# Moving the softmax broadcast matmul behind the next block's first score matmuls, and sharing the feature-major writes between two queues

## The chip, the cores and the metric

The kernel runs on the 8 cores of one Trainium2 chip (two dies, cores 0 to 3 and 4 to 7). The four sequences of the batch are spread over four pairs of cores; each core computes 2048 of the 4096 rows of its sequence, through both layers. No core waits for another. The time is device microseconds of the slowest core.

## The reference, cut to what matters

```python
# x: (4, 4096, 4096)
# attention: 32 heads of 128, 8 key/value heads; every linear is y = x @ sign(W).T * mean|W|
scores = einsum('bhqd,bhkd->bhqk', q, k) / sqrt(128)
attn = softmax(scores, axis=-1)
out = einsum('bhqk,bhkd->bhqd', attn, v)
x = layernorm(x + bitnet_linear(out, o_weight, o_scale))
# feed forward: a base linear and a gated LoRA (8 experts, top 2)
x = layernorm(x + base(x) + 2.0 * lora(x))
```

## The kernel before

The program is a list of stages, each a block in which all engines start together. Stage 1 loads and transposes x. Stage 2 is the Q projection, stage 3/4 the K and V projections, stage 5 the attention, stage 6 the output projection, stage 7 a layernorm, stage 8 the gate and the base linear, stage 9 the last layernorm. Order within a stage is written out by hand with semaphores.

**Attention (`phase5`).** The work is 32 heads times 4 query tiles of 512, which makes 128 blocks, numbered i. Four heads share a key/value head. In a block TensorE goes through 16 steps p of 256 keys. A step issues two score matmuls (line 1123, into one half of the four PSUM banks PSQ), then, for the step before, two value matmuls (line 1217, accumulated in PSA) and two column sums (line 1223, stationary operand a column of ones, accumulated in row 0 of PSD). ScalarE turns each step's scores into a bf16 tile of exponentials (line 1191, three tiles PT in turn). When the last column sum is done, ScalarE computes 1/sum as exp(-ln(sum)) in two small instructions (lines 1195 and 1197), TensorE spreads this row over 128 partitions with a matmul against a row of ones (line 1140, written into PSD as well), VectorE copies the result out of PSD (line 1169) and multiplies PSA by it (line 1171), and GpSimd issues the write to AOUT (line 1205). At the end of a head, VectorE then copies the next head's softmax offset `sm_negu` out of the first half of PSB (line 1176); the first exponential of a new head waits for that copy (`sNg`).

Semaphores of the boundary between blocks: `sPV` counts column sums, `sRc` the reciprocals, `sBc` the broadcast matmuls, `sAo` the products of line 1171, `sEx` the exponentials, `sQK` the score pairs. The first value matmul of a block waits for `sAo` of the block before, because it overwrites PSA. TensorE executes in the order in which the code issues: the score matmuls of block i+1 stand behind the broadcast of block i.

**Layernorm (`emit_ln`).** It runs over 16 tiles of 128 rows. SyncE loads the projection's output and the residual (lines 1260 and 1261) two tiles ahead, once the tile before in the same buffer has been normalized and its write has landed. VectorE adds (1269), takes statistics (1276, 1273, 1279, 1281), waits for ScalarE's square root (1307) and normalizes (1289). In stage 7 only (`fm_out`), ScalarE then casts the tile to bf16 (1312), TensorE transposes it in 32 pieces (1328), VectorE copies four groups of eight out of PSUM (1298), and GpSimd issues one write of the tile to X1TM (1357) and 32 writes of 32 KB each, rows of 256 bytes, to X1FM (1342). Stage 8 begins by loading X1FM (1394), when all of stage 7 is done.

Of the kernel before, what the change touches and what calls it, by code (L numbers as in the profile page):

```python
# [10 lines left out]
AF = mybir.ActivationFunctionType  # L11
# [7 lines left out]
H = 32  # L19
HK = 8  # L20
HD = 128
ND = 32
NTS = 32
NT = 16
# [1036 lines left out]
def phase5(c):  # L1061
# [25 lines left out]
    with nc.Block() as blk:  # L1087
# [16 lines left out]
        def _(t):  # L1104
# [3 lines left out]
            for kvh in range(HK):  # L1108
                bk = kvh % 2
                sKV.wait(t, kvh, per=32)  # L1110
                for r in range(4):
# [3 lines left out]
                    for qt in range(NQT):  # L1115
                        i = h * 4 + qt
                        for p in range(NP):
# [9 lines left out]
                            last.then_inc(sQK, 1)  # L1127
                            if p >= 1:
                                _p5_pvden(c, t, i, p - 1, bk, VBUF, PT, psa, psd,
                                          sEx, sPV, sAo)  # L1130
                            if qt == 3 and p == 4 and h + 1 < H:
# [5 lines left out]
                        _p5_pvden(c, t, i, NP - 1, bk, VBUF, PT, psa, psd, sEx, sPV, sAo)  # L1137
                        t.wait_ge(sRc, i + 1)
                        t.wait_ge(sAo, i)
                        t.matmul(psd[:, 0:512], c.sm_ones_row.ap(),  # L1140
                                 c.sm_recb.ap(), start=True, stop=True).then_inc(sBc, 1)
# [38 lines left out]
        def _(s):  # L1180
            for h in range(H):
                for qt in range(NQT):
# [12 lines left out]
                    sc_(c, s.activation(c.sm_recl.ap(), psd[0:1, 0:512], AF.Ln))  # L1195
# [15 lines left out]
def _p5_pvden(c, t, i, p, bk, VBUF, PT, psa, psd, sEx, sPV, sAo):  # L1211
    t.wait_ge(sEx, NP * i + p + 1)
    if p == 0:
        t.wait_ge(sAo, i)
    for u in range(2):
        cc = 2 * p + u
        t.matmul(psa[:, 0:512], VBUF[bk][:, cc * 128:(cc + 1) * 128],  # L1217
                 PT[p % 3][:, u * 512:(u + 1) * 512],
                 start=(cc == 0), stop=(cc == 31))
    last = None  # L1220
    for u in range(2):
        cc = 2 * p + u
        last = t.matmul(psd[0:1, 0:512], c.sm_ones_col.ap(),  # L1223
                        PT[p % 3][:, u * 512:(u + 1) * 512],
                        start=(cc == 0), stop=(cc == 31))
    last.then_inc(sPV, 1)


def emit_ln(c, name, in_a_dram, in_b_getter, out_writer, fm_out):
# [7 lines left out]
    sCst = _sem(c, name + "_cs")  # L1237
    sTp = _sem(c, name + "_tp")
    sEv = _sem(c, name + "_ev")
    sFd = DSem(c, name + "_fd")  # L1240
# [9 lines left out]
    with nc.Block() as blk:  # L1250
# [13 lines left out]
        def _(v):  # L1264
            for tc in range(NT):
# [25 lines left out]
                if fm_out:  # L1291
                    for g in range(4):
# [3 lines left out]
                        if tc >= 2 and g == 0:  # L1296
                            sFd.wait(v, tc - 2, per=512)
# [5 lines left out]
        def _(s):  # L1303
            for tc in range(NT):
# [3 lines left out]
                if fm_out:  # L1308
# [3 lines left out]
                    s.activation(XB16[b], XB[b], AF.Copy).then_inc(sCst, 1)  # L1312

# [20 lines left out]
        def _(g):  # L1334
            for tc in range(NT):
# [3 lines left out]
                if fm_out:  # L1339
                    g.wait_ge(sEv, 4 * (tc + 1))  # L1340
                    for dc in range(ND):
# [5 lines left out]
            if fm_out:  # L1347
                sFd.wait(g, NT - 2, per=512)
                sFd.wait(g, NT - 1, per=512)
# [184 lines left out]
```

## Time and profile before

| | us |
|---|---|
| median of 2 runs | 10725.3 |
| the two runs | 10706.13 and 10744.47 |
| the profiled execution, its own time | 10707.58 |
| its span, slowest core (core 6) | 10706.0 |
| spans of cores 0 to 3 | 10611.9 to 10621.7 |
| spans of cores 4 to 7 | 10689.9 to 10706.0 |

In the profile PE is TensorE's matmuls, PEld its weight loads, DVE is VectorE, ACT is ScalarE, POOL is GpSimd, SP is SyncE. An engine's busy time on matmuls is modelled, so a busy PE is not PE at its peak. [...] TensorE's matmuls are busy for 76% of the span, ScalarE is busy for 29%, VectorE for 22%, GpSimd for 12%. Times of rows are microseconds from the start of the span of core 6.

### The profile page before, as it was taken

The page shows a single profiled execution, that of the slowest core. Times are in us where ns is not written, and L with a number is a line of the kernel's source. Part 1 is how long each engine was busy: PE and PEld are TensorE (multiplying, and loading weights), DVE is VectorE, ACT ScalarE, POOL GpSimd, SP SyncE. Part 2 cuts the span into 40 slices and gives each one's busy share as a digit, 9 for nine tenths or more (in the row PEclk, how much of TensorE's full clock was granted, in tenths as well). Part 3 has the DMA queues.
Part 4 walks back from the last instruction along what each step waited for, and adds up shares of the span by engine and source line. Part 5 has one row for each costly group of instructions (what it writes and reads, how often), then busy time and mean ns, then how long its engine had stood idle before and what let it go on. Part 6 is the DMA issues. An engine that isn't in the chain of part 4 may idle for free. (4 is left out here: it accounts for less than half of the span.)

```text
span 10706.0 us, 101056 instructions; the slowest of 8 cores (10611.9 to 10706.0 us)
## 1 busy us (share of the span) xinstructions
PE 8146.9 (76%) x35416; PEld 3093.4 (29%) x36044; DVE 2334.5 (22%) x4091; ACT 3083.4 (29%) x2857; POOL 1233.8 (12%) x2278
## 2 busy tenths in 40 slices
PE   3688884888878888888888888867777612899960
PEld 2344432333321111111111111124444311444430
DVE  3344435122210000000000000013333263122226
ACT  3211102000036666665565666620000010111100
POOL 0000000222210000000000000001111173122210
PEclk6799995988888888887888888878888855999975
DMA  9422214111100000000000000032222284222238
GB/s 300 149 69 69 69 56 137 42 42 42 42 27 17 8 17 9 19 16 8 17 8 17 8 17 11 6 104 71 71 71 71 84 304 170 93 83 83 83 115 299
DMA packets 186183, 782.94 MB, mean 73 GB/s; under 512 B 47850, under 2 KB 48226, under 8 KB 158818
## 3 DMA queue, kind: packets, MB, share of 16 engines
q1 hardware_dynamic: 100130, 541.40, 16.0%
q0 software_dynamic: 85568, 235.03, 5.9%
q8 instruction: 310, 5.08, 0.2%
q14 instruction: 175, 1.43, 0.0%
HBM read 541.36 MB, written 234.89 MB: 73 GB/s over the span
## 5 line engine op out<-in xcount | busy, mean ns | idle before, releaser
L552 PE MATMUL PSQ<-BIG 128*128 128x512 bf16 x12000 | 2759.8, 391 | 27.3 <-issue 15.0
L1191 ACT ACTIVATE BIG<-PSQ,sm_negu 128x1024 bf16<-128x1024 f32 x2048 | 2265.7, 1113 | 1364.0 <-PE PSQ L1123 1277.3
L552 PEld LDWEIGHTS PSQ<-BIG 128*128 128x128 bf16 x12288 | 1239.1, 101 | 1532.3 <-issue 265.3
L1217 PE MATMUL PSA<-BIG 128*128 128x512 bf16 x3982 | 1317.4, 412 | 199.4 <-ACT BIG L1191 190.6
L1123 PE MATMUL PSQ<-BIG 128*128 128x512 bf16 x3964 | 1342.5, 428 | 27.1 <-issue 15.1
L523 ACT ACTIVATE BIG<-BIG 128x1024 bf16<-128x1024 f32 x384 | 398.2, 1054 | 3340.0 <-PE PSB L539 2501.4
L1223 PE MATMUL PSD<-BIG,sm_ones_col 128*1 128x512 bf16 x4096 | 1313.6, 404 | 11.1 <-issue 2.7
L1169 DVE CAST BIG<-PSD 128x512 bf16<-128x512 f32 x128 | 88.5, 691 | 3786.6 <-PE PSD L1140 3786.6
L1217 PEld LDWEIGHTS PSA<-BIG 128*128 128x128 bf16 x4096 | 312.3, 101 | 984.6 <-issue 934.7
L539 PE MATMUL PSB<-sm_idb,BIG 128*128 128x128 bf16 x3072 | 259.6, 247 | 401.6 <-DVE BIG L583 310.5
L1123 PEld LDWEIGHTS PSQ<-BIG 128*128 128x128 bf16 x4096 | 257.1, 101 | 968.9 <-issue 960.0
L1205 POOL DMA_DIRECT2D AOUT<-BIG x128 | 69.0, 539 | 3926.4 <-DVE BIG L1171 3893.9
L1223 PEld LDWEIGHTS PSD<-BIG,sm_ones_col 128*1 128x1 bf16 x4096 | 174.9, 81 | 986.2 <-issue 986.2
L928 PE MATMUL PSQ<-BIG 128*128 128x512 bf16 x1024 | 406.2, 397 | 12.7 <-DMA BIG<-XFM 8.3
L636 POOL DMA_DIRECT2D OOUT<-BIG x512 | 271.4, 538 | 1208.7 <-DVE BIG L738 1171.5
L932 PE MATMUL PSQ<-BIG 128*128 128x512 bf16 x1024 | 403.4, 394 | 2.7 <-issue 0.4
L636 POOL DMA_DIRECT2D FFOUT<-BIG x512 | 271.4, 538 | 1150.4 <-DVE BIG L738 1106.4
L926 PE MATMUL PSQ<-BIG 128*128 128x512 bf16 x976 | 387.4, 397 | 4.9 <-DVE BIG L986 4.8
L930 PE MATMUL PSQ<-BIG 128*128 128x512 bf16 x981 | 387.2, 395 | 0.0
L1191 ACT ACT_TABLE_LOAD x1 | 1.3, 1283 | 1264.8 <-PE PSQ L1123 1264.8
L539 PEld LDWEIGHTS PSB<-sm_idb,BIG 128*128 128x128 bf16 x3072 | 221.1, 111 | 447.1 <-issue 427.2
L1328 PE MATMUL PSB<-sm_idb,BIG 128*128 128x128 bf16 x512 | 59.2, 308 | 339.3 <-ACT BIG L1312 336.9
(167 smaller groups left out, 4954.7 us busy)
## 6 DMA issues: line engine op xcount, KB each, us to landing
BIG<-x SPq DMA_DIRECT2D x48, 2048.0 KB, 15.3
BIG<-wq SPq DMA_DIRECT2D x128, 512.0 KB, 5.5
BIG<-wo SPq DMA_DIRECT2D x128, 512.0 KB, 5.3
BIG<-wb SPq DMA_DIRECT2D x128, 512.0 KB, 5.3
XFM<-BIG POOLq DMA_DIRECT2D x32, 1024.0 KB, 14.9
BIG<-XFM SPq DMA_DIRECT2D x32, 1024.0 KB, 4.7
OOUT<-BIG POOLq DMA_DIRECT2D x512, 64.0 KB, 1.9
BIG<-OOUT SPq DMA_DIRECT2D x16, 2048.0 KB, 9.4
```

The lines of the kernel that those rows point to most:

```text
L523: P.inc(s.activation(WSG[i % 4], WST[i % 4], func), "sg")
L539: last = t.transpose(pb[:, j * 128:(j + 1) * 128], WSG[i % 4][:, j * 128:(j + 1) * 128], c.sm_idb.ap())
L552: last = t.matmul(psq[:, qt * 512:(qt + 1) * 512], WT[bdo][:, dc, :], c.RES[:, dc, qt * 512:(qt + 1) * 512], start=(dc == 0), stop=(dc == ...
L636: g.dma_start(out_dram.ap()[tc, :, do * 128:(do + 1) * 128], OSTG[b][:, j * 128:(j + 1) * 128]).then_inc(sDm.h(oq), 16)
L926: t.matmul(psq[:, 0:512], lhs, WKT[:, dc, 0:512], start=(dc == 0), stop=(dc == ND - 1))
L928: t.matmul(psq[:, 512:1024], lhs, WKT[:, dc, 512:1024], start=(dc == 0), stop=(dc == ND - 1))
L930: t.matmul(psq[:, 1024:1536], lhs, WVT[:, dc, 0:512], start=(dc == 0), stop=(dc == ND - 1))
L932: lastmm = t.matmul(psq[:, 1536:2048], lhs, WVT[:, dc, 512:1024], start=(dc == 0), stop=(dc == ND - 1))
L1123: last = t.matmul(psq[:, (cc % 4) * 512:(cc % 4) * 512 + 512], KBUF[bk][:, cc * 128:(cc + 1) * 128], QBUF[bq][:, qt * 512:(qt + 1) * 512], ...
L1191: s.activation(PT[p % 3], psq[:, bank:bank + 1024], AF.Exp, bias=c.sm_negu.ap()[:, h % 2:h % 2 + 1]).then_inc(sEx, 1)
L1217: t.matmul(psa[:, 0:512], VBUF[bk][:, cc * 128:(cc + 1) * 128], PT[p % 3][:, u * 512:(u + 1) * 512], start=(cc == 0), stop=(cc == 31))
L1223: last = t.matmul(psd[0:1, 0:512], c.sm_ones_col.ap(), PT[p % 3][:, u * 512:(u + 1) * 512], start=(cc == 0), stop=(cc == 31))
```

## The change

In attention the broadcast matmul of block i is issued after the first two score matmuls of block i+1, and only the last block keeps it at its end. The column sums move from row 0 of PSD to row 0 of the second half of PSB, from where ScalarE now reads them; the first value matmul of a block gets one more wait, for the reciprocal of the block before, because the column sums that follow overwrite that row. The broadcast still goes to PSD.

In stage 7 the 32 writes of a tile to X1FM are shared: GpSimd issues the even ones and ScalarE, on its own queue and after its cast of the tile and VectorE's four copies, the odd ones. ScalarE's have a semaphore pair of their own (`sFd2`).

```diff
@@ phase5, TensorE
                             last.then_inc(sQK, 1)
+                            if p == 0 and i >= 1:
+                                t.wait_ge(sRc, i)
+                                t.wait_ge(sAo, i - 1)
+                                t.matmul(psd[:, 0:512], c.sm_ones_row.ap(),
+                                         c.sm_recb.ap(), start=True,
+                                         stop=True).then_inc(sBc, 1)
                             if p >= 1:
                                 _p5_pvden(c, t, i, p - 1, bk, VBUF, PT, psa, psd,
-                                          sEx, sPV, sAo)
+                                          sEx, sPV, sAo, sRc)
...
-                        t.wait_ge(sRc, i + 1)
-                        t.wait_ge(sAo, i)
-                        t.matmul(psd[:, 0:512], c.sm_ones_row.ap(),
-                                 c.sm_recb.ap(), start=True, stop=True).then_inc(sBc, 1)
+                        if i == H * NQT - 1:
+                            t.wait_ge(sRc, i + 1)
+                            t.wait_ge(sAo, i)
+                            t.matmul(psd[:, 0:512], c.sm_ones_row.ap(),
+                                     c.sm_recb.ap(), start=True,
+                                     stop=True).then_inc(sBc, 1)
@@ phase5, ScalarE
-                    sc_(c, s.activation(c.sm_recl.ap(), psd[0:1, 0:512], AF.Ln))
+                    sc_(c, s.activation(c.sm_recl.ap(), c.psbf[0:1, 512:1024], AF.Ln))
@@ _p5_pvden
     if p == 0:
         t.wait_ge(sAo, i)
+        if i >= 1:
+            t.wait_ge(sRc, i)
...
-        last = t.matmul(psd[0:1, 0:512], c.sm_ones_col.ap(),
+        last = t.matmul(c.psbf[0:1, 512:1024], c.sm_ones_col.ap(),
@@ emit_ln, ScalarE
                     s.activation(XB16[b], XB[b], AF.Copy).then_inc(sCst, 1)
+                    s.wait_ge(sEv, 4 * (tc + 1))
+                    for dc in range(1, ND, 2):
+                        s.dma_start(c.X1FM.ap()[dc, :, tc * 128:(tc + 1) * 128],
+                                    XSTG[b].rearrange("p (a b) -> p a b", a=32)[:, dc, :]
+                                    ).then_inc(sFd2.h(tc), 16)
@@ emit_ln, GpSimd
-                    for dc in range(ND):
+                    for dc in range(0, ND, 2):
                         g.dma_start(c.X1FM.ap()[dc, :, tc * 128:(tc + 1) * 128],
...
```

## Rows read from the trace of the kernel before

**Rows 1.** Busy time of attention: stretch, us, engines' busy (x count), PEclk, DMA share, GB/s.
```profile
3070.00:6990.00 3920.00, 3482.29 (x12010) 747.12 (x12253) 181.01 (x343) 2384.59 (x2269) 67.41 (x125) 0.87 0.04 13
```
**Rows 2.** Line 1195, one per block: duration min/median/max, first and last start.
```profile
L1195 ACT ACTIVATE BIG<-PSD x128: 586/586/587, 3104.7 to 7049.5; 1x512 f32<-1x512 f32 x128
```
**Rows 3.** Timeline: start, us, instruction [idle before <-releaser], boundary inside a head.
```profile
3283.94 0.59 ACT L1195 ACTIVATE BIG<-PSD 1x512 f32<-1x512 f32 x1 [1.36 <-PE PSD L1223]
...
3285.49 0.37 PE L1140 MATMUL PSD<-BIG,sm_ones_row 1*128 1x512 bf16 x1 [1.65 <-ACT BIG L1197]
3285.80 1.06 PE L1123 MATMUL PSQ<-BIG 128*128 128x512 bf16 x4
...
3286.55 2.12 ACT L1191 ACTIVATE BIG<-PSQ,sm_negu 128x1024 bf16<-128x1024 f32 x2 [1.31 <-PE PSQ L1123]
3286.90 0.69 DVE L1171 TENSOR_TENSOR BIG<-PSA,BIG 128x512 bf16<-128x512 f32 x1
...
3287.92 1.01 PE L1217 MATMUL PSA<-BIG 128*128 128x512 bf16 x2 [1.07 <-ACT BIG L1191]
```
**Rows 4.** Timeline, boundary between two heads.
```profile
3190.88 0.59 ACT L1195 ACTIVATE BIG<-PSD 1x512 f32<-1x512 f32 x1 [1.36 <-PE PSD L1223]
...
3194.75 2.12 ACT L1191 ACTIVATE BIG<-PSQ,sm_negu 128x1024 bf16<-128x1024 f32 x2 [2.56 <-DVE sm_negu L1176]
...
3196.12 1.01 PE L1217 MATMUL PSA<-BIG 128*128 128x512 bf16 x2 [2.34 <-ACT BIG L1191]
```
**Rows 5.** Busy time of five blocks, from one line 1195 to the next.
```profile
3104.70:3132.80 28.10, 24.82 (x95) 5.48 (x97) 1.38 (x2) 18.91 (x18) 0.54 (x1) 1.00 0.02 5
3132.80:3162.70 29.90, 26.22 (x95) 5.75 (x97) 1.58 (x4) 18.97 (x19) 0.54 (x1) 0.94 0.02 5
3162.70:3190.90 28.20, 24.73 (x96) 5.60 (x98) 1.38 (x2) 18.88 (x19) 0.54 (x1) 1.00 0.07 23
3190.90:3222.70 31.80, 27.03 (x95) 5.74 (x97) 1.45 (x3) 18.96 (x19) 0.54 (x1) 0.89 0.02 6
...
3284.00:3314.70 30.70, 27.30 (x96) 5.96 (x98) 1.38 (x2) 18.85 (x19) 0.54 (x1) 0.89 0.07 18
```
**Rows 6.** Busy time within the block of rows 3.
```profile
3287.30:3294.10 6.80, 6.18 (x15) 1.25 (x16) 0.29 (x1) 2.84 (x4) 0.54 (x1) 0.54 0.05 19
```
**Rows 7.** Busy time of one attention block and of two stretches of attention.
```profile
5789.10:5823.00 33.90, 30.18 (x101) 6.62 (x103) 1.45 (x3) 19.85 (x19) 0.54 (x1) 0.81 0.22 82
4774.00:5103.00 329.00, 294.08 (x937) 64.41 (x956) 14.42 (x27) 186.23 (x178) 5.39 (x10) 0.78 0.05 16
5739.00:5898.00 159.00, 142.76 (x464) 31.18 (x472) 7.38 (x15) 92.00 (x89) 2.69 (x5) 0.80 0.06 21
```
**Rows 8.** Timeline of a tile of stage 7.
```profile
8708.62 3.62 ACT L1312 ACTIVATE BIG<-BIG 128x4096 bf16<-128x4096 f32 x1 [3.20 <-DVE BIG L1289]
...
8712.81 0.54 POOL L1357 DMA_DIRECT2D X1TM<-BIG  x1
...
8716.48 0.69 DVE L1298 COPY BIG<-PSB 128x1024 bf16<-128x1024 bf16 x1 [0.16 <-PE PSB L1328]
8717.71 18.89 POOL L1342 DMA_DIRECT2D X1FM<-BIG  x32 [4.36 <-DVE BIG L1298]
8718.27 4.42 DVE L1269 TENSOR_TENSOR BIG<-BIG 128x4096 f32<-128x4096 f32 x1 [1.10 <-DMA BIG<-x]
...
8728.48 0.20 ACT L1307 ACTIVATE sm_sd<-sm_var 128x1 f32<-128x1 f32 x1 [16.24 <-DVE sm_var L1281]
```
**Rows 9.** Waits in stage 7: who waited for whom, us in total, times, longest.
```profile
DVE BIG L1269 <- DMA BIG<-x: 38.5, 12, 25.9
```
**Rows 10.** Lines 1260 and 1394, issues on the SP queue: ns min/median/max.
```profile
L1260 SPq DMA_DIRECT2D BIG<-OOUT x16: 326/327/424, 8541.2 to 8888.0; - x16
L1394 SPq DMA_DIRECT2D BIG<-X1FM x32: 327/1106/3383, 8949.9 to 8986.1; - x32
```
**Rows 11.** Timeline, end of stage 7.
```profile
8926.02 17.08 POOL L1342 DMA_DIRECT2D X1FM<-BIG  x32 [2.76 <-DVE BIG L1298]
```

More of the change, by code:

```diff
@@ L1136, in _ @@
                                          start=True, stop=True).then_inc(sBm, 1)
-                        _p5_pvden(c, t, i, NP - 1, bk, VBUF, PT, psa, psd, sEx, sPV, sAo)
-                        t.wait_ge(sRc, i + 1)
-                        t.wait_ge(sAo, i)
-                        t.matmul(psd[:, 0:512], c.sm_ones_row.ap(),
-                                 c.sm_recb.ap(), start=True, stop=True).then_inc(sBc, 1)
+                        _p5_pvden(c, t, i, NP - 1, bk, VBUF, PT, psa, psd,
+                                  sEx, sPV, sAo, sRc)
+                        if i == H * NQT - 1:
[4 more added lines that the diff above has]
+                                     stop=True).then_inc(sBc, 1)
         @blk.vector
@@ L1208, in _, with _p5_pvden @@
             sAd.wait(g, H * NQT - 1)
-def _p5_pvden(c, t, i, p, bk, VBUF, PT, psa, psd, sEx, sPV, sAo):
+def _p5_pvden(c, t, i, p, bk, VBUF, PT, psa, psd, sEx, sPV, sAo, sRc):
     t.wait_ge(sEx, NP * i + p + 1)
@@ L1236, in emit_ln @@
     sOd = DSem(c, name + "_od")
[L1237 to L1240, printed above, removed]
+    if fm_out:
+        sCst = _sem(c, name + "_cs")
+        sTp = _sem(c, name + "_tp")
+        sEv = _sem(c, name + "_ev")
+        sFd = DSem(c, name + "_fd")
+        sFd2 = DSem(c, name + "_fd2")
+    else:
+        sCst = sTp = sEv = sFd = sFd2 = None
     big1f = c.BIG1.ap().bitcast(F32)
@@ L1296, in _ @@
                         if tc >= 2 and g == 0:
-                            sFd.wait(v, tc - 2, per=512)
+                            sFd.wait(v, tc - 2, per=256)
+                            sFd2.wait(v, tc - 2, per=256)
                         v.tensor_copy(XSTG[b].rearrange("p (a b) -> p a b", a=32)
@@ L1347, in _ @@
             if fm_out:
-                sFd.wait(g, NT - 2, per=512)
-                sFd.wait(g, NT - 1, per=512)
+                sFd.wait(g, NT - 2, per=256)
+                sFd.wait(g, NT - 1, per=256)
+                sFd2.wait(g, NT - 2, per=256)
+                sFd2.wait(g, NT - 1, per=256)
 def phase7(c):
```

## The prediction

> **What bounds the kernel now.** I read the granted clock and busy time by stretch first. Attention takes 3.9 of the 10.7 ms, and its mean granted clock is only 0.87 [rows 1]. TensorE issues 96 matmuls in each block, and line 1195, which runs once per block, starts first at 3104.7 and last at 7049.5 [rows 2]. That is 3944.8 us over 127 blocks, 31.06 us each.
>
> The timeline of a boundary shows what interrupts TensorE. Counted from the start of line 1195, the broadcast starts at +1.55, after 1.65 us of idle. The four score matmuls of two steps run from +1.86. The first value matmul starts at +3.98, after another 1.07 us of idle, and its releaser is the exponential of step 0 [rows 3].  At a boundary between heads the first exponential waits for `sm_negu`, starts at +3.87 instead of +2.61, and the first value matmul starts at +5.24 [rows 4].
>
> The reader should then look at what the pause costs beyond itself. Two blocks ran wholly at 1.00 and took 28.1 and 28.2 us. One at a mean of 0.94 took 29.9. Those at 0.89 took 30.7, or 31.8 at a head boundary [rows 5]. [...] What TensorE did before the fall was to run four large matmuls in 4.2 us. So a boundary costs about 2.5 us through the clock (30.7 less 28.2), beside its waits. All but a handful of the 128 boundaries look like this: at 28.1 us each the 127 blocks would take 3569 us, not 3945.
>
> On this core there is a third kind of block. In 488 us of attention the mean was 0.78 and 0.80, and a block took 33.9 us [rows 7], which makes some 14 blocks 3.3 us longer than the others. That is 46 us, over half of the 84 us by which core 6 ends after the last of cores 0 to 3 (the table above).
>
> **The broadcast moved.** In TensorE's order the score pair of step 0 now comes ahead of the broadcast, right behind the last column sums. Nothing in its own waits holds it back: all exponentials it needs are done. It takes half of the 1.06 us that four score matmuls take [rows 3] and lies in what was 1.65 us of idle. The broadcast itself waits for the same reciprocal, so it stays at +1.55. Behind it only one score pair is left, then the first value matmul.
>
> The first exponential can now start when ScalarE has finished the reciprocal, a little before the broadcast, at about +1.35 instead of +2.61, and it lasts 1.1 us. But the value matmul also waits for `sAo`, since it overwrites PSA. The product of line 1171 starts at +2.96 and lasts 0.69, so it ends at +3.65 [rows 3], and its chain (reciprocal, broadcast, copy, product) is untouched. In this block the value matmul started 0.33 us after that. An engine wakes 0.16 us after its releaser at the shortest [rows 8], and after the exponential TensorE took some 0.3. So the direct gain here is 0.03 to 0.17 us, not the 1.3 us by which the exponential is earlier. [...] The bounds are 0 and 0.5 us; I take 0.2. At the 31 head boundaries the chain through line 1176 stands as it was, and I take 0. Direct gain: 96 blocks by 0.2 is 19 us.
>
> **What the clock makes of it.** The large matmuls of a boundary are the same four, but two of them now join the burst before it. The stretch without a large matmul before the broadcast shrinks from 1.96 us (the last column sum ended 1.65 us before the broadcast, the score matmuls start at +1.86) to about 1.4, while the one before the value matmul grows from 1.07 to about 1.4. The rows show that the fall is not certain even before: of the first three boundaries, all with the same pauses, two had none [rows 5]. Where the stretch of 4.2 us is better filled at its front, more boundaries should pass without a fall, and those that fall should do so later, when TensorE is already in its dense work again and can leave the low level sooner, as the block at 0.94 did. [...] The bounds for one inner block are 0 (all fall as now) and 2.5 us (30.7 less 28.2, none falls). I take one half without a fall (2.5) and one half with the short one (30.7 less 29.9, 0.8), a mean of 1.65 us. This includes most of the direct gain. At head boundaries TensorE idles 2.34 us before the value matmul [rows 4] as before, and I take no gain. Of the 96 inner blocks about 11 lie in the stretches of rows 7, where I take nothing either. That leaves 85 by 1.65, which is 140 us.
>
> **The sums' new row** costs nothing: the same matmuls write another bank, and the added wait for `sRc` is already met when the broadcast has gone. Its cover is the broadcast's own wait; without that it would be the 1.3 us of the reciprocal, which cannot come after it.
>
> **The shared writes of stage 7.** A tile has a cycle of 23 us, set by VectorE. GpSimd needs 18.89 us to issue 32 writes. This delays the next tile's X1TM write: it is issued at 8712.81, though ScalarE had the normalized tile at 8708.62, and the loads that wait for it come late: VectorE waited 1.10 us in this tile [rows 8]. All such waits of the stage are 38.5 us, of which 25.9 are the first tile's, leaving 12.6 [rows 9]. With 16 writes GpSimd is free 9.4 us earlier, so I take 10 of them. At the end the last 32 writes are issued from 8926.02 to 8943.1, [rows 11], and stage 8's loads start at 8949.9 [rows 10]; half of the issuing goes, 8 us.
>
> On ScalarE the 16 issues go between the last copy (end 8717.17) and the square root at 8728.48 [rows 8], 11.3 us in which ScalarE was idle. Behind them waits exactly that square root, and VectorE for it. No row shows an issue by ScalarE. The nearest are SyncE's: 0.33 us each, where few are under way, and a median of 1.11 for 32 in a row of 512 KB each [rows 10]. With about 0.05 between two issues that makes 6 or 18.5 us. I take the low end, since these writes are 32 KB; then nothing is late. At the high end each tile is 7.2 us late. Stage 7: minus 18 us.
>
> [...]
>
> **Sum.** 10,707.6 (the profiled execution) less 140 less 18 is 10,550. That execution lies 18 us under the median of the two runs, 10,725.3, and their spread is 38 us.
>
> **Rivals.**
> - *Every boundary falls as before (0.20).* For it: the same four large matmuls in the same 4.2 us, and VectorE's chain holds the value matmul near +3.9. Against: 2 of 3 early boundaries passed. Left are 19 us and stage 7's 18: 10,670.
> - *No inner block falls (0.18).* 85 by 2.5 is 213, and stage 7's 18: 10,477, over 2% faster than the median.
> - *ScalarE's issues are slow (0.09).* 7.2 us for 15 tiles is 108 us on top of 10,550, less the 10 that are no longer gained: 10,668.
> - *The third level spreads (0.10), the slower side.* Denser work on all cores of the die makes blocks like that of rows 7 more frequent. Each costs 33.9 less 29.2, some 4.7 us against a block of the new kind. From 30 more of them on, the 140 us are gone. If half of all blocks are such, 50 more, the time is 10,785. For it: 0.81 appears on this core in 488 us of attention already. Against: it fills only an eighth of attention, and blocks shortened from 30.7 to 29 us are denser by no more than 6%. [...]
> - *The forecast (0.43).*
>
> **Range and chances.** 2% is about what a measurement of this kernel tells from no change, here 215 us, so faster begins at 10,511. The range is 10,455 to 10,705: it takes in the first three rivals and leaves out most of the fourth and the edges. The forecast's own range is 10,490 to 10,610. Faster: the 0.18 and a tenth from the forecast's lower edge, 0.26. Slower by over 2% would need 10,940, some 80 blocks at the third level: 0.03. Within 2%: 0.71.
>
> **What would show it.** In the profile after: line 1171, not line 1191, releases the first value matmul inside a head, and its start is about +3.9 after line 1195. Blocks of 28 us at a mean of 1.00 stand between others of 29.5 to 30 us; the mean granted clock of attention rises from 0.87 to 0.92 or so, and line 1195's first and last start lie some 3800 us apart. In stage 7 VectorE hardly waits for loads, ScalarE's last issue ends before the next square root is due, and from the stage's start to line 1394 there are about 18 us less. What would make it wrong: a clock that still falls in each block, or stretches at 0.81 over more than a third of attention.

## The result and the profile after

| us | before | after |
|---|---|---|
| median | 10768.26 (9 runs) | 10707.67 (11 runs) |
| lowest and highest | 10701.34 and 10994.81 | 10552.39 and 10860.95 |
| profiled execution, span of its slowest core | 10706.0 (core 6) | 10551.1 (core 1) |
| attention on that core, first to last logarithm | 3944.8 | 3788.5 |
| stage 7 on that core, first addition to the first load of stage 8 | 392.3 | 438.8 |

The ratio of after to before is 0.9833, with a 95% interval of 0.978 to 0.9885; it is taken over the fast runs alone, those in which no die lagged behind the other and whose time lay near the kernel's fastest, while the medians of the table are over all runs (their ratio is 0.9944). Even that ratio is not all the change's. All nine runs of the kernel before took over 10,700 us, and its profiled execution spent time at the clock level of 0.81 [rows 7]. Core 1 of that execution had no such time and took 10,621.7 us, the kernel's fastest later runs took 10,621.6 to 10,628.7, and four of after's eleven took 10,552.4 to 10,558.9, a ratio of 0.9935. So of the 1.7% about 0.65% is shown to be the change itself; the rest most likely goes with that level.

The logarithm, once per block (columns: duration ns min/median/max, first and last start), stands for [rows 2]: 3788.5 us over 127 blocks, 29.83 each, where there were 31.06.

```profile
L1204 ACT ACTIVATE BIG<-PSB x128: 586/586/587, 3107.8 to 6896.3; 1x512 f32<-1x512 f32 x128
```

Busy time by stretch of after (us, PE, PEld, DVE, ACT, POOL with counts, PEclk, which is the clock granted to TensorE as a share of full speed, DMA share, GB/s): attention, which answers to [rows 1], then stage 7.

```profile
3070.00:6990.00 3920.00, 3418.56 (x12589) 733.13 (x12590) 193.66 (x362) 2429.79 (x2313) 69.06 (x128) 0.93 0.06 19
8405.30:8844.10 438.80, 59.10 (x512) 51.58 (x512) 243.29 (x288) 62.39 (x33) 144.15 (x272) 0.52 0.74 258
```

The mean granted clock of attention went from 0.87 to 0.93. Five blocks of after, from one logarithm to the next, answer to [rows 5]:

```profile
3224.80:3252.80 28.00, 25.06 (x98) 5.39 (x97) 1.38 (x2) 18.89 (x18) 0.54 (x1) 1.00 0.02 6
3252.80:3282.40 29.60, 26.59 (x98) 5.58 (x97) 1.58 (x4) 18.91 (x18) 0.54 (x1) 0.94 0.02 5
3310.60:3342.70 32.10, 27.73 (x98) 5.77 (x97) 1.45 (x3) 18.91 (x18) 0.54 (x1) 0.89 0.19 75
3342.70:3373.50 30.80, 27.86 (x98) 5.77 (x97) 1.38 (x2) 18.94 (x19) 0.54 (x1) 0.89 0.01 5
3373.50:3404.20 30.70, 27.76 (x98) 5.77 (x97) 1.58 (x4) 18.89 (x19) 0.54 (x1) 0.89 0.01 5
```

The same three kinds stand here as before: 28.0 us at 1.00, 29.6 at 0.94, 30.7 at 0.89, and a head boundary with 32.1. Only their shares changed. I counted over all 127 blocks of a core how many held a stretch at a granted clock of 0.50. Before it was 125 to 127, and nearly all of these stretches were long ones (6.8 us, as in rows 6). After, on core 1, 48 blocks held none, 30 a short one (half of that) and 49 a long one. All 48 without one are inner blocks; of the 31 blocks that begin with a head boundary 10 had a short one and 21 a long one. The kinds do not come at random: on this core the same order of them (five long, none, short, none, two short, two none) comes back several times, and the counts of five other cores are the same or differ by one.

The timeline of a boundary inside a head of after answers to [rows 3]:

```profile
3224.79 0.59 ACT L1204 ACTIVATE BIG<-PSB 1x512 f32<-1x512 f32 x1 [1.36 <-PE PSB L1234]
...
3226.00 1.09 ACT L1200 ACTIVATE BIG<-PSQ,sm_negu 128x1024 bf16<-128x1024 f32 x1
...
3226.34 0.37 PE L1131 MATMUL PSD<-BIG,sm_ones_row 1*128 1x512 bf16 x1 [1.11 <-ACT BIG L1206]
...
3227.41 1.11 ACT L1200 ACTIVATE BIG<-PSQ,sm_negu 128x1024 bf16<-128x1024 f32 x1 [0.32 <-PE PSQ L1123]
3227.75 0.69 DVE L1180 TENSOR_TENSOR BIG<-PSA,BIG 128x512 bf16<-128x512 f32 x1
3228.70 0.59 PE L1228 MATMUL PSA<-BIG 128*128 128x512 bf16 x2 [1.44 <-ACT BIG L1200]
```

Counted from the logarithm, the broadcast starts at +1.55 as before, the first exponential at +1.21 instead of +2.61, and the first value matmul at +3.91. The row names an exponential as releaser, but the one that this matmul reads had ended at 3227.09, 1.6 us earlier, and the one named is the next (the row of 3227.41), which ended at 3228.52; the product ended at 3228.44, 0.26 us before the matmul. Idle ahead of the broadcast is 1.11 us instead of 1.65, and ahead of the value matmul 1.44 instead of 1.07.

In stage 7 the waits (who waited for whom: us in total, times, longest) and the groups of the shared writes and of the first addition and the stage 8 loads (duration ns, first and last start) are:

```profile
ACT sm_sd L1323 <- issue: 275.9, 14, 20.5
DVE sm_rstd L1299 <- ACT sm_sd L1323: 72.7, 16, 5.9
DVE BIG L1284 <- DMA BIG<-x: 26.2, 1, 26.2
```

```profile
L1331 ACTq DMA_DIRECT2D X1FM<-BIG x256: 326/526/5776, 8428.6 to 8832.3; - x128
...
L1284 DVE TENSOR_TENSOR BIG<-BIG x32: 4415/4422/4427, 8405.3 to 10528.9; 128x4096 f32<-128x4096 f32 x32
...
L1417 SPq DMA_DIRECT2D BIG<-X1FM x32: 326/1090/2348, 8844.1 to 8879.5; - x32
```

VectorE no longer waits for loads after the first tile (26.2 us in one wait, where [rows 9] have 12), but it now waits 72.7 us for ScalarE's square root, where the same waits of the kernel before are:

```profile
DVE sm_rstd L1284 <- ACT sm_sd L1307: 7.6, 16, 1.7
```

The timeline of one tile of after, beside [rows 8], shows why:

```profile
8563.10 4.42 DVE L1284 TENSOR_TENSOR BIG<-BIG 128x4096 f32<-128x4096 f32 x1
8563.26 13.76 ACTq L1331 DMA_DIRECT2D X1FM<-BIG  x16
8563.71 8.47 POOL L1363 DMA_DIRECT2D X1FM<-BIG  x16 [8.33 <-DVE BIG L1314]
...
8573.04 0.15 DVE L1296 TENSOR_SCALAR sm_var<-sm_mv 128x1 f32<-128x1 f32 x1
8577.12 0.20 ACT L1323 ACTIVATE sm_sd<-sm_var 128x1 f32<-128x1 f32 x1 [19.04 <-issue]
8577.43 0.16 DVE L1299 RECIPROCAL sm_rstd<-sm_sd 128x1 f32<-128x1 f32 x1 [4.23 <-ACT sm_sd L1323]
```

The variance was ready at 8573.19, but ScalarE issued writes until 8577.02. GpSimd had done its 16 in 8.47 us.

**The accounting.** From core 6 of before to core 1 of after the span fell by 155 us (10706.0 less 10551.1). Attention gave 156 (3944.8 less 3788.5) and stage 7 took 47 (438.8 less 392.3). From stage 8's loads to the end there are 1756.1 us before [rows 10] and 1707.0 after, 49 less, though nothing was changed there: the kernel before had two stretches at 0.81 in it on that core. The remaining 4 us are the stages ahead of attention and between it and stage 7, which took that much longer. Core 1 of the same execution of before had no such stretches: its attention took 3897.3, so the change gave 109 there and not 156, and its span went from 10621.7 to 10551.1, 71 less.

### The profile page after: what moved, and what is told of

Same layout as the page of the kernel before. It is cut to its first block and busy times, and to the rows that moved or that the text cites. A ratio compares the mean times of both kernels' runs of the same rounds, so it can differ in the third digit from the quotient of the medians.

```text
span 10551.1 us, 101843 instructions; the slowest of 8 cores (10533.7 to 10551.1 us)
## 1 busy us (share of the span) xinstructions
PE 7985.2 (76%) x36044; PEld 3037.9 (29%) x36044; DVE 2334.3 (22%) x4091; ACT 3082.7 (29%) x2857; POOL 1071.0 (10%) x2022
## 5 line engine op out<-in xcount | busy, mean ns | idle before, releaser
L552 PEld LDWEIGHTS PSQ<-BIG 128*128 128x128 bf16 x12288 | 1229.7, 100 | 1499.8 <-issue 123.9
L1228 PE MATMUL PSA<-BIG 128*128 128x512 bf16 x4096 | 1284.4, 396 | 287.3 <-ACT BIG L1200 285.6
L1234 PE MATMUL PSB<-BIG,sm_ones_col 128*1 128x512 bf16 x4096 | 1270.3, 393 | 0.0
L1123 PEld LDWEIGHTS PSQ<-BIG 128*128 128x128 bf16 x4096 | 235.1, 98 | 921.7 <-issue 921.3
L1234 PEld LDWEIGHTS PSB<-BIG,sm_ones_col 128*1 128x1 bf16 x4096 | 174.8, 81 | 930.9 <-issue 930.9
```

What stands on the lines that cost most here:

```text
L552: last = t.matmul(psq[:, qt * 512:(qt + 1) * 512], WT[bdo][:, dc, :], c.RES[:, dc, qt * 512:(qt + 1) * 512], start=(dc == 0), stop=(dc == ...
L1123: last = t.matmul(psq[:, (cc % 4) * 512:(cc % 4) * 512 + 512], KBUF[bk][:, cc * 128:(cc + 1) * 128], QBUF[bq][:, qt * 512:(qt + 1) * 512], ...
L1234: last = t.matmul(c.psbf[0:1, 512:1024], c.sm_ones_col.ap(), PT[p % 3][:, u * 512:(u + 1) * 512], start=(cc == 0), stop=(cc == 31))
```

## Experiments

In the expectations A is my theory: the boundary costs through the clock, and through the waits only a little. D is the theory that only the waits themselves count. "Cores without 0.81" are those whose attention held no stretch at that level; attention is always taken from the first to the last logarithm.

**Each half by itself.** First attention as in the change with stage 7 as before:

```diff
-                    s.wait_ge(sEv, 4 * (tc + 1))
-                    for dc in range(1, ND, 2):
-                        s.dma_start(c.X1FM.ap()[dc, :, ...
-                    for dc in range(0, ND, 2):
+                    for dc in range(ND):
```

> The changed kernel with stage 7 as it was before: GpSimd issues all 32 writes of a tile to X1FM, ScalarE none; attention as changed. Theory A (ScalarE's 16 issues per tile hold up the square root): stage 7 goes back from 439 us to about 391 us, attention keeps 3788 us from the first to the last logarithm, and an undisturbed core ends 48 us sooner than with the whole change, near 10,503. Rival B (stage 7 became longer because of something the attention part left behind, such as the moment at which it starts beside the other cores): stage 7 stays near 439 us and the time near 10,551.

Its fastest run took 10,508.7 us. Attention took 3777 to 3795 us with 78 to 82 falls of the clock, as in after (cores without 0.81), and stage 7 took 389 to 399, so B falls. The other half, attention as before and stage 7 as in the change:

> The kernel before with only the shared writes of stage 7. Theory A: stage 7 is 439 us instead of 391, attention is 3890 to 3902 us on undisturbed cores as before, and an undisturbed core ends at 10,621 plus 48, near 10,670: slower than before. Rival C (the shared writes are neutral and what made the time is attention alone): 10,621 on undisturbed cores.

Its fastest run took 10,666.9 us (ratio to before 1.0064, interval 0.9988 to 1.0139). Attention took 3895 to 3901 with 127 falls. C falls. Its rows for the first addition, the loads of stage 8 and ScalarE's writes:

```profile
L1273 DVE TENSOR_TENSOR BIG<-BIG x32: 4412/4420/4426, 8518.4 to 10643.1; 128x4096 f32<-128x4096 f32 x32
...
L1406 SPq DMA_DIRECT2D BIG<-X1FM x32: 326/1047/3880, 8957.7 to 8993.5; - x32
...
L1320 ACTq DMA_DIRECT2D X1FM<-BIG x256: 326/527/5609, 8541.7 to 8945.9; - x128
```

8957.7 less 8518.4 is 439.3 us, as in after (436.5 to 442.4 on its cores). So the halves add up: against 10,621.6, the fastest run of the kernel before, attention alone brings 113 us, stage 7 alone costs 45, and both together, at 10,552.4, bring 69.

**Only the new row of the sums and the added wait**, with the broadcast back at the end of its block:

```diff
-                            if p == 0 and i >= 1:
-                                t.wait_ge(sRc, i)
-                                ... (the broadcast)
-                        if i == H * NQT - 1:
+                        if True:
                             t.wait_ge(sRc, i + 1)
```

> Of the attention part only the new place of the column sums (PSB instead of PSD) and the added wait; the broadcast stays at the end of its block as before; stage 7 as before. Theory A: neutral, attention 3890 to 3902 us on undisturbed cores, a clock fall at nearly every boundary, 10,620 for an undisturbed core. Rival E (freeing PSD is what shortens the boundary, the order is not): attention near 3788 us and 10,503.

The logarithms (columns as above):

```profile
L1198 ACT ACTIVATE BIG<-PSB x128: 587/587/588, 3106.7 to 7014.7; 1x512 f32<-1x512 f32 x128
```

3908.0 us, 10,628.3 for the whole, and a fall in 126 or 127 of the 127 blocks. So E falls, and the gain is the moved broadcast's. The row and the wait are not quite free: against before's 3891 to 3902 they cost some 10 us, 0.1 us a block. (In the trace of after the added wait is an instruction of its own between the product's end and the value matmul, 0.1 us behind the wait for the product.)

**The broadcast behind two score pairs** instead of one:

```diff
-                            if p == 0 and i >= 1:
+                            if p == 1 and i >= 1:
                                 t.wait_ge(sRc, i)
```

> Attention as changed, but the broadcast stands behind the score matmuls of steps 0 and 1 of the next block, not of step 0 alone; stage 7 as before. Theory A (the waits of a boundary are held by VectorE's product, and what is gained or lost comes through the clock): the first value matmul still starts 3.9 us after the logarithm, a block without a fall of the clock is still 28.1 us, but the stretch between the last score matmul and the first value matmul becomes one pause of 3 us, after which the clock falls more often: a mean block of 29.9 us instead of 29.8 and attention 3790 to 3830 us. Rival D (what counts is the wait before the broadcast, which holds more matmuls now): attention 40 to 60 us shorter than with one pair, about 3735 us.

The logarithms:

```profile
L1204 ACT ACTIVATE BIG<-PSB x128: 587/587/588, 3106.0 to 6888.9; 1x512 f32<-1x512 f32 x128
```

Attention took 3772 to 3783 us, 10,497.6 for the fastest run. That is just below what A gave (3790 to 3830) and far from D's 3735. The falls rose to between 87 and 90, as A had it, but more of them were short, which it had not: on core 3, whose logarithms stand above, 38 blocks without one, 58 short, 31 long. The second pair neither helps nor hurts by an amount worth having.

**The offset of the next head copied before the broadcast's result**, so that no chain of VectorE's stands before the first exponential of a head (attention else as in the change, stage 7 as before):

```diff
+                    if qt == 3 and h + 1 < H:
+                        hn = h + 1
+                        v.wait_ge(sBm, hn + 1)
+                        v.tensor_copy(c.sm_negu.ap()[:, hn % 2:hn % 2 + 1],
+                                      c.psbf[:, 0:1]).then_inc(sNg, 1)
                     v.wait_ge(sBc, i + 1)
...
-                    if qt == 3 and h + 1 < H:
-                        ... (the same copy)
```

> Attention as changed, and VectorE copies the next head's offset out of PSUM before it waits for the broadcast of the head's last block, not after its product; stage 7 as before. Theory A: the first value matmul of a head starts 3.9 instead of 5.3 us after the logarithm. The blocks at head boundaries, 31.6 us on average, become like the others. If these keep their mixture of falls, the mean block is 28.7 us and attention 3650 us; if every block settles at the length of a block with a long fall, 30.7 us each, it is 3900 us. Rival D (only waits count, the clock is not moved by them): 31 times 1.35 us, 42 us less than 3788, attention 3746 us.

The logarithms, and busy time of attention with the granted clock (the third number from the end):

```profile
L1204 ACT ACTIVATE BIG<-PSB x128: 586/587/588, 3109.7 to 6772.4; 1x512 f32<-1x512 f32 x128
```

```profile
3105.00:6767.00 3662.00, 3278.00 (x12348) 702.80 (x12347) 186.70 (x347) 2402.61 (x2287) 68.51 (x127) 0.97 0.04 14
```

3662.7 us, 126 less than after's 3788.5 (A gave 3650, D 3746), and the whole at 10,381.5 in its fastest run, 127 less than the 10,508.7 of the first experiment, which has the same stage 7 (ratio to before 0.9728, interval 0.9548 to 0.9908). At the 31 head boundaries the value matmul now starts at +3.91 instead of +5.34. That is 1.4 us, or 44 us for all of them. D can have no more than that. The other 82 us came with the clock: 57 falls instead of 79, none of them long (five on core 5), and 70 blocks without one. With the head boundaries short, hardly a long fall is left at an inner one either, though nothing was changed there; that the first set off the second is likely by this, but no run moved it alone.

**The value matmul freed of the product as well**, by two accumulators taken in turn, PSA and PSD, with the broadcast in PSB, on top of the edit before:

```diff
-    psa = c.PSA.ap()
-    psd = c.PSD.ap()
+    psa2 = [c.PSA.ap(), c.PSD.ap()]
+    psd = c.psbf
...
     if p == 0:
-        t.wait_ge(sAo, i)
+        if i >= 2:
+            t.wait_ge(sAo, i - 1)
```

> On top of the early offset: the value matmuls of even and odd blocks accumulate in two PSUM banks (PSA and PSD) and the broadcast goes to the first half of PSB, so that the first value matmul no longer waits for VectorE's product of the block before. Theory A: it starts when the first exponential is done, at about 2.7 us after the logarithm instead of 3.9, a block without a fall takes 26.95 us, and most of the 57 falls that the early offset left disappear, since the last pause shrinks from 1.5 to 0.4 us: attention about 3460 us. Rival D (waits only): 127 times 1.2, 152 us less than 3663, attention 3511 us. Rival F (the product is not what the value matmul waits for): 3663 us.

On core 1, as the logarithms and the busy time of attention:

```profile
L1206 ACT ACTIVATE BIG<-PSB x128: 587/587/588, 3100.3 to 6517.6; 1x512 f32<-1x512 f32 x128
```

```profile
3110.00:6525.00 3415.00, 3185.81 (x12319) 687.41 (x12318) 186.73 (x347) 2400.70 (x2281) 68.50 (x127) 1.00 0.04 14
```

The value matmul starts at +2.66. That settles who held it at +3.91: the product, as its wait is the only one that was taken away (the broadcast also changed its bank and got a wait more). F falls. Attention takes 3417.3 us, 26.9 a block, where A gave 3460 and D 3511, and on the cores of die 0 the clock fell at most three times in the whole of it. Die 0 ended at 10,122 to 10,134 us. Die 1 did not (span and mean granted clock):

```profile
core 1: 10134.2 us, clock 0.882
...
die 0 (median of its cores): 10128.1 us, clock 0.882
die 1 (median of its cores): 10551.5 us, clock 0.830
```

It spent some 3 ms at 0.81 and had 11 to 14 falls in attention, and the fastest run of six took 10,271.3.

**More work in the pause.** The first experiment's kernel (attention as in the change, stage 7 as before), with four matmuls more at each boundary whose output is thrown away (the broadcast overwrites it):

```diff
                             if p == 0 and i >= 1:
-                                t.wait_ge(sRc, i)
                                 t.wait_ge(sAo, i - 1)
+                                for _f in range(4):
+                                    t.matmul(psd[:, 0:512],
+                                             KBUF[bk][:, _f * 128:(_f + 1) * 128],
+                                             QBUF[bq][:, qt * 512:(qt + 1) * 512],
+                                             start=True, stop=True)
+                                t.wait_ge(sRc, i)
```

> Attention as changed, stage 7 as before, and between the score matmuls of step 0 and the broadcast four more matmuls of 128x512 whose results nobody reads (the broadcast overwrites them): 508 matmuls more, all in the 1.3 us in which TensorE waits for the reciprocal. No wait becomes shorter. Theory A (the clock falls because of the pauses): fewer falls than 79, blocks of 28.1 us at inner boundaries twice as often, attention 3680 to 3740 us in place of 3788. Rival D (only the waits count): attention 3788 us or more, since work is only added.

This separates the clock from every theory that counts work and waits alone, for by those 508 matmuls more can't make a kernel faster. The value matmul starts 0.1 us earlier (+3.81), which for 127 boundaries is 13 us at most. In the profiled execution both dies had stretches at 0.81, yet cores 4 and 5 took 3721 and 3719 us for attention with 0.15 ms of it at that level (3777 to 3795 without the four), inside A's 3680 to 3740. The eight cores had 47 to 55 falls instead of 78 to 82. The logarithms of core 5, then the busy time of its attention and that of core 1 of the first experiment's kernel, which has the same attention without the four:

```profile
L1209 ACT ACTIVATE BIG<-PSB x128: 587/587/587, 3279.1 to 6998.0; 1x512 f32<-1x512 f32 x128
```

```profile
3279.00:6998.00 3719.00, 3416.31 (x12859) 758.23 (x12858) 183.85 (x347) 2403.89 (x2287) 68.53 (x127) 0.96 0.04 13
...
3105.00:6900.00 3795.00, 3367.83 (x12350) 714.40 (x12350) 183.81 (x347) 2403.61 (x2286) 68.52 (x127) 0.94 0.04 13
```

In two of its four runs a die kept a mean clock of 0.874 and ended at 10,405 and 10,406 us (median of its cores), against 10,491 to 10,511 for the five dies that were undisturbed without the four: at least 84 us, of which the earlier value matmul explains no more than 13. D falls. The time of the slowest core does not show this gain. All four runs had a pair of cores at 0.81 (10,543.2 to 10,964.6 us), where the fastest without the four took 10,508.7, in another session.

**The pause taken away.** The steps of all blocks run as one sequence: the scores of a block's first step stand before the last value matmuls of the block before, the reciprocal stands behind the first exponential, and the broadcast two steps later. Attention is otherwise as with the two accumulators, stage 7 as before.

```diff
+            for g in range(NP * H * NQT + 1):
+                i, p = g // NP, g % NP
...
-                            if p == 0 and i >= 1:
+                    if p == 2 and i >= 1:
                         t.wait_ge(sRc, i)
...
+                if g >= 1:
+                    j, q = (g - 1) // NP, (g - 1) % NP
+                    _p5_pvden(c, t, j, q, (j // 16) % 2, VBUF, PT, psa2[j % 2],
+                              sEx, sPV, sAo, lnb)
@@ ScalarE
+                if p == 0 and i >= 1:
+                    recip(i - 1)
```

> On top of the two accumulators: blocks run into each other. The score matmuls of the next block's step 0 are issued ahead of the value matmuls of this block's step 15, ScalarE computes that step's exponentials before the logarithm, and the broadcast comes in step 2 of the next block; stage 7 as before. Theory A: TensorE has no pause over 0.5 us at a boundary, the clock does not fall in attention, and a block is 16 steps of 1.53 us and the broadcast, 24.8 us: attention about 3150 us, 9,870 for an undisturbed core. Rival H (without the pauses the die goes to the level of 0.81 and stays there, where a step takes 1.77 us): 28.6 us per block, attention about 3630 us, no better than with the early offset. Rival I (ScalarE becomes the bound, 16 exponentials of 1.11 us, two small ones and their latencies): over 27 us per block.

On core 7:

```profile
L1190 ACT ACTIVATE BIG<-PSB x128: 569/570/587, 3103.1 to 6306.1; 1x512 f32<-1x512 f32 x128
```

Attention took 3203 us on cores without 0.81, 25.2 a block (A gave 3150 and 24.8), with no fall at all, and up to 3333 on others. But all cores of the profiled execution did have that level somewhere, for 2.1 to 2.7 ms, and they ended at 10,218.9 to 10,307.8; the fastest of four runs took 10,043.4, and cores without the level ended at 9,900 to 9,918. H falls: the level comes, but it does not stay, and it does not take the gain back. I falls.

**ScalarE's share of the writes.** Eight of 32 instead of 16, the rest as in the change:

```diff
-                    for dc in range(1, ND, 2):
+                    for dc in range(3, ND, 4):
...
-                    for dc in range(0, ND, 2):
+                    for dc in [x for x in range(ND) if x % 4 != 3]:
```

> The changed kernel, but ScalarE issues 8 of a tile's 32 writes to X1FM and GpSimd 24. In the changed kernel ScalarE's first nine issues of a tile take 0.3 to 1.1 us each, the tenth 4.5 to 5.8 us, while the last two tiles, beside which no loads run, have no such stall and take 7 us for all 16. Theory A1 (the queue takes about nine writes until the first has landed, and what makes the square root late is the tenth): with 8 there is no stall, the issues take 5 to 6 us, the square root is on time, stage 7 takes 375 to 385 us, less than the 391 of before, and an undisturbed core ends near 10,495. Rival A2 (each issue by ScalarE is slow by itself, 0.86 us on average): also on time with 8, but then the issues take 7 us evenly. Rival G (the transfers of ScalarE's queue slow down the loads): stage 7 stays above 400 us.

The groups of ScalarE's writes, of the first addition and of the stage 8 loads, and VectorE's wait for the square root:

```profile
L1331 ACTq DMA_DIRECT2D X1FM<-BIG x128: 326/516/1069, 8423.0 to 8768.8; - x128
...
L1284 DVE TENSOR_TENSOR BIG<-BIG x32: 4415/4424/4427, 8399.7 to 10478.7; 128x4096 f32<-128x4096 f32 x32
...
L1417 SPq DMA_DIRECT2D BIG<-X1FM x32: 327/1052/3129, 8788.5 to 8824.1; - x32
```

```profile
DVE sm_rstd L1299 <- ACT sm_sd L1323: 7.6, 16, 1.7
```

Stage 7 takes 388.8 us on this core (384 to 395 on the eight), and the fastest run took 10,502.5. No issue is longer than 1.07 us (2.0 on the worst core), where 16 in a row had one of up to 5.8 in nearly every tile, and VectorE's wait for the square root is 7.6 us again. A2 and G fall. A1 has the stall right, but its 375 to 385 us for the stage did not come. Twelve of 32, in one profiled execution, show where the step is:

```diff
-                    for dc in range(1, ND, 2):
+                    for dc in [x for x in range(ND) if x % 8 in (1, 4, 7)]:
```

> The changed kernel, ScalarE issues 12 of a tile's 32 writes to X1FM and GpSimd 20. Theory A1 (the queue takes about nine before the first has landed): the tenth stalls for about 5 us, the twelve take 11 to 12 us, the square root is 0 to 1 us late, stage 7 near 400 us. Rival A2 (slow by itself, 0.86 us each): no single long issue.

ScalarE's writes in it:

```profile
L1331 ACTq DMA_DIRECT2D X1FM<-BIG x192: 326/542/6718, 8397.2 to 8773.7; - x192
```

The tile's twelve issues took 12.6 us in the median (core 6), of which the tenth took 4.1 to 6.7; stage 7 took 409 to 417 and VectorE's wait for the square root 48 to 50 us, both more than A1 gave. The run's time was 10,666.2, with the level of 0.81 on six cores. So the stall sits at a place in the row and does not shrink with ScalarE's share: with eight nothing stalls, with twelve the tenth does, by as much as with 16. What it waits for is less sure. In after the first of a tile's writes landed 10.9 us behind its issue in the median of the first 14 tiles (core 1) and the tenth issue ended at 10.5, which fits A1's "until the first has landed", but in the tile shown above it ended 0.7 us before that landing.

**Both together**: the one sequence of blocks and ScalarE's eight writes.

> The pipelined attention with 8 of 32 writes issued by ScalarE in stage 7. An undisturbed die: 9,904 less 2 to 5 us, 9,900, against 10,610 of the kernel before; where a die is at the level of 0.81 up to 400 us more. Theory A sees the same 127 blocks of about 25 us with no fall; a rival in which ScalarE's queue disturbs stage 7 as in the changed kernel would give 9,950.

On core 1, the logarithms and the busy time of attention:

```profile
L1190 ACT ACTIVATE BIG<-PSB x128: 570/570/587, 3103.7 to 6306.9; 1x512 f32<-1x512 f32 x128
```

```profile
3110.00:6310.00 3200.00, 3177.57 (x12326) 690.24 (x12324) 186.22 (x347) 2369.50 (x2282) 67.97 (x126) 1.00 0.04 15
```

Span and mean granted clock of core 0 and of die 1:

```profile
core 0: 9904.2 us, clock 0.879
...
die 1 (median of its cores): 10267.5 us, clock 0.840
```

TensorE is busy for 3178 of 3200 us, and nothing is left to take from its pauses. Cores 0 and 1 end at 9,904 and 9,914, where 9,900 was expected. The fastest run took 10,044.8, the median of six 10,361.1; in the profiled execution die 1 spent 2.1 to 2.6 ms at 0.81, none of it in attention. It is well ahead of both kernels all the same: every one of its six runs (10,044.8 to 10,545.3) lies under the fastest of after.

## Why the prediction was right, and where it was not

The number, 10,550, is that of the profiled execution (10,552.7), and the chances had most of their weight on a small gain, which is what came. But that the number was met is luck. The sum had 158 us to gain, of which the change itself gave 71 (core 1). The other 84 of the 155 between the two slowest cores lie in the base: core 6 of before had lost time to the level of 0.81, which after's execution did not meet. One term had the wrong sign, and a gain was in the result that the sum did not contain. By its steps:

- **The bound** was read rightly. A boundary costs through the clock. In the block of [rows 6] it was 0.50 for 6.8 us from 3286.68 on, +2.74 after the logarithm. Ahead of that lie 2.8 us since the last column sum, with the broadcast and the four score matmuls in them, and not the 4.2 us of the prediction. More work in the pause made undisturbed dies at least 84 us faster, and without the pause 127 blocks run at 1.00.
- **Who holds the value matmul.** The product, as forecast, at +3.9; the forecast that the profile would name it was wrong, as it named an exponential that merely ended at the same moment. The direct gain was put at 0.2 us, an estimate that no run shows, and was 0.47 to 0.53: over all inner boundaries the value matmul started at +4.38 to +4.44 before (median), and [rows 3] with +3.98 was one of the boundaries at which the clock was still up when the score matmuls started. The upper bound, 0.5, was for the case that turned out to be the usual one: on core 1 of before the first score matmul already ran at 0.50 at 54 of the 96 inner boundaries. At the one whose logarithm starts at 3105.77 the four score matmuls took 1.89 us instead of the 1.06 of [rows 3]: most matmuls of 512 columns that stand in a row start 0.43 us apart at 0.50 and 0.22 at 1.00, which makes 0.42 us for a pair. The first exponential came at +3.26 instead of +2.61, and it held the value matmul until +4.62.
- **The clock.** A mixture came, with the three kinds of blocks that were named. For the 96 inner blocks half without a fall and half with a short one were taken; 48 without, 20 short and 28 long came. So the half without was right and the long kind was left out. The mean inner block went from 30.54 to 29.23 us (core 1), 126 us for 96 of them, in place of the 140; less the 17 of the next item, attention gave 109. The argument for the weights was weaker than it looked: of core 6's 127 blocks before, the two without a fall in [rows 5] were the only two. The long kind did not get shorter although its value matmul starts earlier: those blocks take 30.7 us as before, so what the front of the block saved was spent at the low level.
- **Head boundaries** were put at 0. The value matmul there went from +5.24 to +5.34, and the blocks that begin with one from 31.14 to 31.68 us in the mean (core 1), 17 us for 31. The larger mistake was to see nothing in them: [rows 4] had the longest idle time of any boundary, and curing it later brought 126 us, more than the whole change.
- **The sums' new row** was put at nothing. It and its wait cost about 0.1 us a block.
- **Stage 7** is the step that failed: minus 18 was forecast and plus 47 came. The cost of an issue on ScalarE had been bounded from SyncE's rows at 6 to 18.5 us for 16, and I took the low end, because these writes are small. They took 14.5 us in the median, 3.2 more than the 11.3 that were free. The rest of the reasoning held: it was the square root that waited and VectorE behind it, 72.7 us where it had been 7.6. The gains that I had counted were there too and are in the sum: 65 more for the square root, 12 less for loads and 5.5 less at the end (the last copy to stage 8's first load took 19.0 us instead of 24.5) make the 47. The rival of slow issues had the mechanism. Its price was 7.2 us a tile; VectorE waited 4.5 in the mean (72.7 over 16). Nor would free issues have brought the 18. With eight writes the stage took 384 to 395 us on the eight cores, against 389 to 399 with stage 7 as before and attention as after, since VectorE then waits again for loads (nine waits, 34.8 us, on core 7).
- **The third level** was left out of the forecast's sum and made up for stage 7. Core 6 of before had lost some 47 us to it in attention (3944.8 less core 1's 3897.3) and 49 behind stage 7, 96 in all, in 0.39 ms of attention and 0.3 ms later; after's profiled execution had none. The 488 us that a rival gives it are the whole of the two stretches of [rows 7], a fifth of which ran at other levels. The forecast took that execution as its base, with both in it. Whoever sets a sum against one execution should ask which part of its time another execution would not have.
- **The chances.** The 0.26 for faster does not follow from its parts: 0.18 and a tenth are 0.28, and 0.18 and a tenth of the forecast's 0.43 are 0.22. No conclusion hangs on it.

TensorE's pauses at a boundary of before were brief, 1.65 and 1.07 us in [rows 3], and the clock fell in 125 to 127 of 127 blocks. On the issues the two sides stand in the tile shown above and in [rows 8]: GpSimd saved 10.4 us a tile (18.89 less 8.47), and ScalarE paid 14.5 for it in the median, in a place where its time was wanted.

What stays open is why of two boundaries with the same pauses in the same kernel one has a fall and the next has not. The counts (127, then 79, 57, and 3 at most on cores without 0.81) go with the pauses, and the order of the kinds repeats itself, so it is no chance; but none of the runs moved the place of a boundary alone.

## What to carry to other kernels

Look at the granted clock at each pause of TensorE, however short, before pricing the pause by its idle time: here two at a boundary, 2.7 us together, cost 2.5 us more through the clock. When DMA issues move to another engine, look at the whole burst in front of that engine's next due instruction and at how many stand in a row, not at the cost of one: here 16 in a row took 14.5 us, of which the tenth alone took 4.5 to 5.8, and eight took 3.7 to 5.8 (core 7). Where a slower level comes and goes, as that of 0.81 did here, take base and result from cores or runs that do not show it, or the sum may meet the time by chance.

## What the runs showed of the hardware that was not expected

- **A stall at the tenth write in a row.** Of 16 writes of 32 KB in a row on ScalarE's queue (after, core 1) the first issue took 0.33 us, the next eight 0.45 to 1.1, the tenth 4.5 to 5.8, and the last ones about 0.45 again. In the last two tiles, with no loads beside them, all 16 took 7.6 us from the first's start to the last's end and none stalled; there the first write had landed after 1.5 us. What the tenth waits for, no run took apart. With eight in a row (the run with ScalarE's share at a quarter) the longest of any tile took 2.0 us. On GpSimd each of the 16 took 0.54 to 0.55 us (after); with 24 or 32 in a row (that run, and before) single ones took up to 2.6.
- **The level of 0.81 comes in some executions and not in others.** A trace counts time from its own core's first instruction, and in the first experiment cores 4 and 5 had eight stretches at 0.81, from 794 us of their spans on, and cores 6 and 7 eight at the same distances from 6972 us on, six of them of the same length within 16 us. In four more executions (of the kernel before and of the last kernels) the stretches of two pairs of a die agree in the same way, shifted by 2.3 to 6.6 ms. So the two pairs seem to meet the same stretches at different places of the same program. What brings the level is not shown. In the last experiment's profiled execution all eight cores ran attention at 1.00, with TensorE 99% busy on core 1, and cores 2 and 3 had 0.77 ms at 0.81 elsewhere while cores 0 and 1 had none.
- **That denser work meets the level more often is not shown.** All 16 runs of the three densest kernels had it (10,043.4 us at the least, where undisturbed cores end by 9,918 us). But in the session of two of these kernels so had all seven runs of the kernel before, up to 11,155.7 us, while the kernel with the early offset had two runs of five without. The rival that denser work would spread the level stays open.
- **What short pauses cost.** TensorE's pauses and the falls that go with them cost 3897 less 3203, that is 694 us of 10,622. What took them away was the order of a few instructions at 127 boundaries and a second accumulator.
